# Attention scores two mLSTM heads sooner, and the routing places in three parts behind heads 12 to 14, in a one-core decoder layer

## What is computed

```
x = LN(x + attn(x))         # 16 heads of 32, 4 key/value heads, half of each head rotated,
                            # softmax(q k^T / sqrt(32)) v, then Wo
x = LN(x + mlstm(x, ctx))   # 16 heads: gates from x and ctx, D = exp(log_fg + i - rowmax) below the
                            # diagonal, C = (x ctx^T / sqrt(32)) * D, divided by max(|sum C|, exp(-rowmax)),
                            # times ctx, normalised per head, times ln_scale
x = LN(x + moe(x))          # 16 experts, top 2 of (logits + bias), shares = softmax over the two,
                            # silu(x Wu) * (x Wg) Wd, and one shared expert
```

## Time and profile before

| | |
|---|---|
| median of 3 runs | 2096.3 us (2095.43 to 2103.06) |
| time of the profiled execution | 2090.95 us |
| span of the profiled execution | 2089.3 us |
| TensorE matmuls, busy | 1871.2 us, 90% of the span |
| VectorE | 1196.6 us, 57% |
| ScalarE | 650.3 us, 31% |
| GpSimd | 696.2 us, 33% |
| granted TensorE clock, mean | 0.951 of full speed |

### The profile page before, as it was taken

The page is one execution under the profiler, slowest core; times in us unless marked ns, Lnnn a source line. Parts: engine busy times, 40 slices in busy tenths (PEclk is TensorE's granted clock), DMA queues, the critical chain, the costliest instruction groups (busy, mean ns, idle before and its releaser), DMA issues. The chain is left out here.

```text
span 2089.3 us, 35576 instructions
## 1 busy us (share of the span) xinstructions
PE 1871.2 (90%) x11010; PEld 1185.8 (57%) x11011; DVE 1196.6 (57%) x2474; ACT 650.3 (31%) x1358; POOL 696.2 (33%) x754
## 2 busy tenths in 40 slices
PE   3879999999999999999999999998879999999990
PEld 2456575766657576665757666575644444444440
DVE  2567777766776776677777667776442222222225
ACT  1142433334243333424333342433302212222224
POOL 3124133332413333241333324133123444444430
PEclk8789999999999999999999999999979999999995
DMA  7153242344424234441423444142324666656549
GB/s 274 44 124 98 56 118 72 90 110 89 118 42 118 72 88 111 89 118 42 118 72 89 111 89 118 41 99 62 105 102 87 134 168 163 148 121 142 90 77 334
DMA packets 151843, 226.92 MB, mean 109 GB/s; under 512 B 32448, under 2 KB 107200, under 8 KB 149056
## 3 DMA queue, kind: packets, MB, share of 16 engines
q1 hardware_dynamic: 101616, 132.94, 24.6%
q0 software_dynamic: 38336, 92.38, 18.4%
q10 hardware_dynamic: 11792, 0.61, 0.4%
HBM read 94.70 MB, written 48.83 MB: 69 GB/s over the span
## 5 line engine op out<-in xcount | busy, mean ns | idle before, releaser
L1575 PE MATMUL ps<-ug_w,rowsT 128*128 x640 | 292.8, 601 | 8.1 <-SPq L1424 4.5
L1575 PEld LDWEIGHTS ps<-ug_w,rowsT 128*128 128x128 f32 x640 | 123.0, 193 | 163.7 <-issue 163.7
L1464 POOL DMA_INDIRECT sum_rows<-y_sb,pairs x80 | 127.3, 1591 | 248.6 <-DVE y_sb L1542 136.5
L869 DVE RECIPROCAL arden<-ps 128x256 f32<-128x256 f32 x64 | 112.5, 1758 | 140.2 <-PE ps L1321 136.6
L1064 PE MATMUL ps<-wqkv_sb,xT_sb 128*128 128x256 f32 (+1 forms) x512 | 172.3, 490 | 15.3 <-ACT maskr_sb L524 15.3
L1530 DVE SCALAR_TENSOR_TENSOR silu<-tanh,ps 128x256 f32<-128x256 f32 x80 | 33.7, 422 | 251.7 <-ACT tanh L1485 251.7
L961 DVE SCALAR_TENSOR_TENSOR weighted<-ps,decay 128x384 f32<-128x384 f32 x256 | 139.2, 553 | 66.4 <-PE ps L1190 50.4
L851 DVE TENSOR_REDUCE smax<-ps 128x2 f32<-128x512 f32 x256 | 164.0, 682 | 16.5 <-PE ps L1247 16.5
L476 POOL DMA_INDIRECT routed_ids<-pair_w,pos_w x64 | 64.0, 1000 | 324.7 <-DVE pair_w L747 288.1
L641 ACT ACTIVATE probs<-ps 128x1024 f32<-128x1024 f32 x128 | 130.8, 1024 | 114.8 <-PE ps L1298 114.8
L620 ACT ACTIVATE decay<-ps,g_col 128x256 f32<-128x256 f32 x256 | 121.3, 474 | 137.5 <-PE ps L1173 90.8
(11 more groups left out here) (253 smaller groups left out, 3835.0 us busy)
## 6 DMA issues: line engine op xcount, KB each, us to landing
q_stack<-qkT_hi SPq DMA_DIRECT2D x128, 128.0 KB, 3.8
mk_stack<-ctxT_hi SPq DMA_DIRECT2D x128, 128.0 KB, 5.1
mq_stack<-qkT_hi SPq DMA_DIRECT2D x128, 128.0 KB, 2.4
ug_w<-in_expert_ug SPq DMA_DIRECT2D x16, 1024.0 KB, 5.3
xT_sb<-in_xT SPq DMA_DIRECT2D x16, 512.0 KB, 3.3
x_sb<-in_x POOLq DMA_DIRECT2D x16, 512.0 KB, 3.8
ctxT_sb<-in_ctxT POOLq DMA_DIRECT2D x16, 512.0 KB, 3.6
q_stack<-qkT_lo SPq DMA_DIRECT2D x64, 128.0 KB, 4.3
```

The costliest lines, as they stand in the source:

```text
L1464: pool.indirect_dma_start(out=sum_dram, out_offset=bass.IndirectOffsetOnAxis(ap=tables.pairs[:, m, 0:1], axis=0), in_=y_sb[:, m % W, :], i ...
L1575: ins = nc.tensor.matmul(ps[:, 2 + k % 2, :], rowsT[:, k % 2, c, :], ug_w[:, bass.ds(slot, 1), c, :].rearrange("p o n -> p (o n)"), start= ...
```

## The change

Three tables of numbers change: scores stand beside heads 4 to 11 instead of 6 to 13, and the maxima are transposed at head 12 instead of 14, now behind that head's `decay_mm(14)` instead of ahead of it. `place_rows` is cut into `place_own`, `place_chosen` and `place_pairs`, behind heads 12, 13 and 14; the shares stand behind head 15, and ScalarE's `exp_gap` behind the decay of head 14. SyncE issues the eight high DMAs of `q_stack` without waiting for the low part, and the maxima's high row without waiting for the low row.

```
-        FIRST_S, MAXIMA_AT = 6, 6 + H // 2
+        FIRST_S, MAXIMA_AT = 4, 4 + H // 2
         FIRST_NUM, FIRST_HID = 10, 13
-        RANKS_AT, PLACES_AT, SHARES_AT = 1, 3, 9
+        RANKS_AT, PLACES_AT, GAP_AT, SHARES_AT = 1, 12, 14, 15
...
             for row, part in enumerate(order):
+                if part is None:
+                    continue
...
                     wait(sp, qk_hi_done, b, 2)
+                    stack(sp, q_stack, qkT_hi, qkT_lo, None, q_in, ("hi", "hi", None))
                     wait(sp, qk_lo_done, b, 2)
-                    stack(sp, q_stack, qkT_hi, qkT_lo, None, q_in, Q_ROWS)
+                    stack(sp, q_stack, qkT_hi, qkT_lo, None, q_in, (None, None, "lo"))
 
                     wait(sp, m_hi_done, b, 1)
+                    sp.dma_start(q_stack[96:97, :, :].bitcast(F32), m_hi[:, :].bitcast(F32)).then_inc(m_in.sem, 16)
                     wait(sp, m_lo_done, b, 1)
-                    for row, src in ((96, m_hi), (97, m_lo)):
-                        sp.dma_start(q_stack[row:row + 1, :, :].bitcast(F32), src[:, :].bitcast(F32))\
-                            .then_inc(m_in.sem, 16)
+                    sp.dma_start(q_stack[97:98, :, :].bitcast(F32), m_lo[:, :].bitcast(F32)).then_inc(m_in.sem, 16)
...
-                        if h == SHARES_AT - 2 and w is not None:
+                        if h == GAP_AT and w is not None:
                             exp_gap()
...
                 def place_rows():
 
-                    step = Steps(dve, place_step, w)
+                    place_own()
+                    place_chosen()
+                    place_pairs()
+
+                step = Steps(dve, place_step, w) if w is not None else None
+
+                def place_own():
                     nc.vector.tensor_tensor(place[:, 0, :], ranks[:, 0, 0, :], filled[:, :], ALU.add)
...
                     nc.vector.tensor_tensor(filled[:, :], filled[:, :], ranks[:, 1, 1, :], ALU.add)
+
+                def place_chosen():
                     step(nc.vector.tensor_tensor(by_k(onehot), by_k(onehot), over_k(place), ALU.mult), rest=rest)
...
                                             best[:, :].unsqueeze(1).to_broadcast([P, TOPK, ST]), ALU.subtract).then_inc(gap_done.sem, 1)
+
+                def place_pairs():
                     wait(dve, pairs_sent, w, 0)
...
                             if w is not None and h == PLACES_AT:
-                                place_rows()
+                                place_own()
+                            if w is not None and h == PLACES_AT + 1:
+                                place_chosen()
+                            if w is not None and h == PLACES_AT + 2:
+                                place_pairs()
                             if w is not None and h == SHARES_AT:
                                 place_shares()
...
                             for k in scored_beside(h):
                                 s_mm(k)
-                            if h == MAXIMA_AT:
-                                transpose_maxima()
                         if h + 2 < H:
                             decay_mm(h + 2)
+                        if b is not None and h == MAXIMA_AT:
+                            transpose_maxima()
```

## The result

| | before | changed |
|---|---|---|
| median of 18 runs each, same chip | 2095.43 us (2086.28 to 2103.06) | 2099.86 us (2097.23 to 2105.15) |
| span of the profiled execution | 2089.3 us | 2099.5 us |
| granted clock, mean | 0.951 | 0.944 |

The ratio is **1.0028 (95% interval 1.0016 to 1.0041)**: 0.3% slower, where 1.0% faster was forecast. By the bound of 0.5% that is no change; it lies outside the range of the forecast. Two more chips repeated it: 1.0033 [1.0017, 1.0049] and 1.0027 [1.0011, 1.0044].

The account below looks back on a forecast made before the run. TensorE bounds the kernel: a turn shortens only where it stands still or lacks its full clock. 14.0 + 3.8 + 1.4 + 6.0 - 4.5 = 20.7 us off, forecast 2075.6 us, range 2066 to 2085 (0.60).

Parts of the forecast that it names:

- (a): Full turn, scores from head 4: the q_stack rows have landed well before head 4 begins, so no new wait.
- (b): Full turn, heads 4 to 11: without place_rows and shares there, eight heads take 15.57 us; head 12 starts at 867.15.
- (c): Full turn from head 12: VectorE's pieces sum to 5.61 us; the last product starts at 873.31, ends at 874.17.
- (d): Full turn's end: the wait for the maxima row goes, true scores start 1.0 us sooner, 14.0 us in fourteen turns.
- the gain is eaten by the chain: Rival, turn's end: routing and maxima take 0.7 us more, a turn gains 0.3, every end stall falls; 2088.4 us; chance 0.17.
- (e): Clock: falls behind place_rows go, 6.0 us won; end falls 12 in 14 instead of 9, 4.5 us lost.
- the clock stays up: Rival, turn's end: the one stall brings no falls, all nine go; 38.7 us less, 2057.6 us; chance 0.15.
- (f): Turn 1, which has no routing: both end waits and the fall behind them go, 3.8 us.
- (g): Turn 0: q_stack begins sooner, 1.0 us, and the maxima's high row goes before the low, 0.4: 1.4 us.
- (h): Behind the shares: GpSimd's four scatters take 5.2 us, to about 879; hidden by 7 us before GpSimd is next needed.
- (i): ScalarE at head 15: the shares' exponential comes ahead of the decay, done at 872.6; costs nothing, but by 0.1 us.
- The slower rival: ScalarE's exponential, waiting for the chosen places, delays head 15's decay; at 2.5 us late 2113.6 us; chance 0.05.

Follow-up runs that it names:

- the exponential moved: The changed kernel with ScalarE's share exponential behind head 15's decay instead of ahead of it: 2102.3 us, ratio 0.9932 to the kernel before.
- the falls filled away: The changed kernel with two dummy fp32 products ahead of the last weighted-value product: 2068.5 us, ratio 0.9875 to the kernel before; 0.9887 on another chip.
- the rows together: The changed kernel with SyncE as before, maxima rows issued together and the q_stack rows behind the low part's wait: 2106.4 us, ratio 0.9956 to the kernel before.
- the pairs last: The changed kernel with place_pairs behind head 15, ahead of the shares, instead of behind head 14: 2070.2 us, ratio 0.9885 to the kernel before.

## Why the prediction was wrong, point by point

- (a) No new wait at head 4: right. Head 4 starts 5.12 us behind the first head, and no wait for its rows comes back turn by turn.
- (b) Head 12 on TensorE: 20.96 us behind the heads' start, 20.70 by the forecast. 0.26 of the 1.0 us a turn lost.
- (c) VectorE's chain: right in kind (nothing but VectorE's own steps in it), short in size: 6.12 us, not 5.61. The own places took 0.99 (0.86 forecast), the chosen 1.43 (1.36), the pairs 0.90 (0.62), the rest 0.03. Another 0.5 us lost. On their old places the next instruction started 0.04 to 0.08 us before the last step of own and chosen ended, and now it starts 0.03 to 0.05 behind. Most of the pairs' 0.28 is the gap of 0.32 us ahead of `weighted` 15; it stays when ScalarE's decay comes 1.4 us sooner, so it isn't ScalarE, and its cause is not shown.
- (d) The wait for the maxima row is gone: right. But of the 1.0 us a turn, (b) and (c) left 0.3 (89.41 against 89.73): **14.0 us forecast, about 4 in the profile**. The rival "the gain is eaten by the chain" named just this, 0.3 a turn, and so did the sign of being wrong: a plain turn not under 89.4 us.
- "What is late next": 2.4 us of standing still were forecast in one wait; 0.68 and 2.05 came, in two.
- **(e) The clock is the step that failed.** Forecast and profile lie 30.9 us apart (20.7 less, 10.2 more): 18.5 of these are falls, 9.8 the true scores' start in (d), 1.4 the first turns, 1.2 the end. The falls of `place_rows` went, as forecast, 6.0 us. The end falls were counted at 12 of 14 and priced at 1.5 us each, 4.5 us more than before. They came in nearly every turn and lasted twice as long, 2.73 us each: 17.0 us were lost by falls where 1.5 were to be gained. The long kind was in sight ("long one", 1.8 over a clean half) but only behind `place_rows`; that the end could bring it was in no case of the forecast. The rival "the clock stays up" went the other way, and the eaten gain's 2088.4 had priced its 14 falls at 1.5.
- (f), (g) The first turns, up to the heads of turn 2: 5.2 forecast, 3.8 came. Turn 0 gave 1.0 (118.97 to 117.93 us at the heads of turn 1) of 1.4, turn 1 gave 2.7 of 3.8.
- (h) The scatters end at 885.7, the variance step starts at 892.96 behind VectorE's `hvar`: hidden, right.
- (i) ScalarE: decay 15 ends at 878.29, `weighted` 15 starts at 878.80 behind the pairs: right, and shown by the experiment with the exponential moved.
- The slower rival was named for ScalarE; what made it slower was the clock. The Trainium skill's rule ("TensorE: Matmul & The Clock Gate", Part 1), by which the clock falls only behind a stretch idled throughout, and which gave 2078.6, does not fit here either: the fall comes within two rows in which TensorE was busy 1.23 and 0.59 of 2.00 us. The same part of that page of the Trainium skill also tells of a kernel whose clock goes up and down because TensorE idles briefly between groups of products, which is nearer to this case; the forecast left it out. With the falls filled away the kernel reads 2068 to 2069 us on chips that read 2092 to 2094 for the kernel before, 24 us off. That does not bear out the 17.7 of the sum without falls: some 19 of the 24 are the falls of the kernel before, and the order of the work gave 4.2 in thirteen turns.

## What to carry to other kernels

Hidden work that is moved to where the busiest engine waits is paid at full, and the steps between it at more than they cost elsewhere. Price a stall by the clock behind it too: half a microsecond less of standing still (2.05 to 1.57 us) took most falls away, 1.4% in all, and four passes a turn that compute nothing gave 1.5%. When a stall can't be removed, a filling shorter than it is worth a try, sized by a measured pass. Before idle time is filled, find out what it is: VectorE's 3.3 us behind its loop's branch could not be. And a ratio holds for the chip that it was measured on: two of six chips added some 20 us to the kernel before, and not to its relatives.

## What the runs showed of the hardware that was not expected

- A fall can last 6.8 us instead of 3.4 at the same stall, with TensorE busy without a gap in 6 of them. Which of the two comes is not set by the length of the waits alone: with 0.68 and 2.05 us of them the fall was long in most turns of the changed kernel and short in most of the one with the exponential moved (on one of the two chips, where the rows together fell long); the kernel before, with 0.74 and 1.51, fell at the end of 9 turns in 14, and the one with the pairs last, with 0.68 and 1.57, had 4 falls in all.
- Turns with a long fall repeat almost exactly (92.13, 92.12, 92.13 us). In its three profiles, from three chips, the changed kernel never left that state once it was in it; with the rows together it did once. That turn and clock lock onto each other is what this looks like; it was not tested.
- An fp32 product of 128x512 is recorded as two passes, which took 0.45 us each (3.6 us for eight).
- The kernel before reads 1% more on two chips of six. In every trace from these two TensorE's results come late beside GpSimd's scatters (a copy 2.23 us behind the start of its transposition instead of 0.69), in 100 of 105 turns, against 12 of 161 in the other traces. Why those chips do it was not found.
- VectorE's queue goes on 2.7 to 3.6 us behind the branch that closes its loop (kernel before, eleven turns; 3.2 to 3.6 in the versions with the routing behind head 15, and 0.04 us or less where `floors` has no branch before it). It costs nothing where VectorE has nothing to do, and holds the averages of every version with the routing behind head 15.
